# GpSimd takes the layernorm application and the residual-plus-bias sum from VectorE in the stages with heads of 8

## The reference, cut to what matters

```
xn = (x - mean(x)) / sqrt(var(x) + 1e-5)             # over the 128 channels
q  = heads(xn @ Wq + bq)                              # 16 heads of 8
k, v = heads(ctx @ Wk + bk), heads(ctx @ Wv + bv)     # 1601 keys
y  = softmax(q k^T / sqrt(8)) v
out = x + y @ Wp + bp
```

## Time and profile before

| | before |
|---|---|
| timed runs, median | 8038.13 us |
| profiled execution | 8022.59 us, span 8020.8 us |
| PE | 7135.1 us busy, 89% |
| DVE | 5918.4 us, 74% |
| ACT | 4951.6 us, 62% |
| POOL | 2313.2 us, 29% |

### The profile page before, as it was taken

How to read it: one execution, slowest core, us unless ns; L and a number is a source line. 1 busy time by engine, 2 the same in 40 slices (tenths; PEclk the granted TensorE clock), 3 DMA queues, 4 the chain that set the end, 5 groups by cost and what they waited for, 6 DMA issues and landing times. The chain is left out here.

```text
span 8020.8 us, 186125 instructions
## 1 busy us (share of the span) xinstructions
PE 7135.1 (89%) x73814; PEld 3142.3 (39%) x73814; DVE 5918.4 (74%) x12885; ACT 4951.6 (62%) x9846; POOL 2313.2 (29%) x2368
## 2 busy tenths in 40 slices
PE   6999999878999997888599999999998779999979
PEld 2333333353333333444244444444444533333335
DVE  6888888657989996677466666666665469899855
ACT  4778887636888884444255555555554248888852
POOL 1222222111121110444245444544444211221200
PEclk9999999888999998788699999999999779999989
DMA  4444333114433421000100000000000144434400
GB/s 97 101 95 92 83 83 92 45 26 100 99 89 77 99 65 31 15 16 13 53 6 8 7 6 10 6 10 6 7 3 18 49 83 96 96 84 85 97 22 14
DMA packets 319828, 417.80 MB, mean 52 GB/s; under 512 B 56533, under 2 KB 238053, under 8 KB 318968
## 3 DMA queue, kind: packets, MB, share of 16 engines
q1 hardware_dynamic: 317432, 405.36, 22.4%
q10 hardware_dynamic: 1536, 0.53, 0.0%
HBM read 225.41 MB, written 174.66 MB: 50 GB/s over the span
## 5 line engine op out<-in xcount | busy, mean ns | idle before, releaser
L687 ACT ACTIVATE a_probs<-scores_ps 128x512 f32<-128x512 f32 (+2 forms) x5248 | 2821.7, 591 | 356.2 <-PE scores_ps L607 263.4
L746 DVE TENSOR_REDUCE a_unit_max<-bank 128x1 f32<-128x512 f32 x3072 | 2004.0, 684 | 182.0 <-PE bank L594 147.3
L624 PE MATMUL bank<-a_probs,a_v_sb 128*9 128x256 f32 (+1 forms) x20992 | 1614.1, 379 | 29.4 <-ACT a_out_sb L694 20.4
L1275 ACT ACTIVATE cross_probs<-scores_ps 128x512 f32<-128x512 f32 (+1 forms) x1792 | 869.4, 571 | 772.6 <-PE scores_ps L1172 772.6
L1357 DVE TENSOR_REDUCE cross_unit_max<-bank 128x1 f32<-128x512 f32 x1536 | 1006.5, 687 | 319.7 <-PE bank L1158 316.9
L607 PE MATMUL scores_ps<-a_stack 64*128 64x256 bf16 (+1 forms) x10496 | 1131.5, 275 | 61.6 <-ACT a_probs L687 55.8
L1441 POOL TENSOR_TENSOR cross_added<-cross_probs 128x1024 f32<-128x1024 f32 x384 | 902.4, 2350 | 944.6 <-PE bank L1205 868.8
L746 DVE TENSOR_REDUCE a_unit_max<-scores_ps 128x1 f32<-128x512 f32 x1536 | 1050.2, 684 | 162.1 <-PE scores_ps L594 144.6
L594 PE MATMUL bank<-a_stack 63*128 63x512 bf16 (+2 forms) x3413 | 1039.7, 372 | 8.1 <-DMA a_stack<-a_stack_dram 2.6
L607 PEld LDWEIGHTS scores_ps<-a_stack 64*128 64x128 bf16 (+1 forms) x10496 | 373.5, 96 | 991.9 <-ACT a_probs L687 832.8
L594 PE MATMUL scores_ps<-a_stack 63*128 63x512 bf16 (+2 forms) x1707 | 635.9, 373 | 50.8 <-DMA a_stack<-a_stack_dram 47.5
(11 more groups left out here) (421 smaller groups left out, 10119.5 us busy)
## 6 DMA issues: line engine op xcount, KB each, us to landing
a_stack_dram<-a_parts SPq DMA_DIRECT2D x288, 400.2 KB, 4.3
a_stack<-a_stack_dram SPq DMA_DIRECT2D x256, 348.2 KB, 8.0
a_stack<-a_stack_dram SPq DMA_DIRECT2D x128, 444.2 KB, 9.9
a_ctxT<-in_ctxT SPq DMA_DIRECT2D x48, 400.2 KB, 4.9
a_stack_dram<-a_parts SPq DMA_DIRECT2D x288, 64.0 KB, 2.7
a_stack_dram<-a_parts SPq DMA_DIRECT2D x96, 128.0 KB, 2.8
f_x<-x_after_dram SPq DMA_DIRECT2D x32, 256.0 KB, 3.6
x_after_dram<-a_res SPq DMA_DIRECT2D x48, 128.0 KB, 4.6
```

The costliest lines, as they stand in the source:

```text
L624: ins = pe.matmul(out_bank[32 * h:32 * h + V8, q0:TOK], v[0:n, e.t, 4 * e.g + h, :], A.probs[0:n, held, o + q0:o + TOK], start=(e.t == 0), ...
L687: act.activation(by_pair(A.probs[0:n, b, a * 512:(a + 1) * 512])[:, :, q0:TOK], by_pair(score_bank[(2 * e.i + a) % 3][0:n, :])[:, :, q0:TO ...
L746: ins = dve.tensor_reduce(unit_max[:, e.g % 2, qt, 2 * a + j, c:c + 1], bank[:, 0:e.s.chunks[c][1]], AX.X, ALU.max)
L1275: act.activation(probs[0:n, b, h, 0:m, :].rearrange("p m q -> p (m q)"), score_bank[h][0:n, 0:m * TOK], ACT.Exp, scale=scale).then_inc(S[" ...
```

## The change

Two things move from VectorE's list to GpSimd's. `ln_apply` (two instructions of 128x128) is issued by GpSimd at the same event, step 4, between its second and its third `split`. The sum of `x_res` and `b_out` (two instructions of 128x128) is issued by GpSimd at the event `heads_turned`, and a new semaphore `x_res_done` tells VectorE of it. VectorE keeps only the last addition of `proj`. GpSimd's wait for `ln_rstd` moves from behind `ln_rstd` to ahead of `ln_apply`.

```diff
-        S = Sems(nc, ctx, stage, ["ones_in", "ahead_in", "x_res_in", "ln_done", "side_ps", "side_done", "part0", "left",
+        S = Sems(nc, ctx, stage, ["ones_in", "ahead_in", "x_res_in", "x_res_done", "ln_done", "side_ps", "side_done", "part0", "left",
...
-                if e.kind == "ln_apply":
-                    dve.wait_ge(S["ln_rstd"], made + 1)
-                    for t in range(QT):
-                        ins = ln_apply(dve, L, t, xn[:, t, :], x_sb[1 - p][:, t, :])
-                    ins.then_inc(S["ln_done"], 1)
...
                 if e.kind == "proj":
-                    dve.wait_ge(S["x_res_in"], 16 * (prev + 1))
                     if prev >= 1:
                         dve.wait_ge(S["x_out"], 16 * prev)
-                    for t in range(QT):
-                        ins = dve.tensor_tensor(x_res[:, t, :], x_res[:, t, :], W_sb["b_out"][:, :], ALU.add)
-                    chain(ins)
+                    dve.wait_ge(S["x_res_done"], prev + 1)
                     dve.wait_ge(S["side_ps"], e.n + 1)
...
                 if e.kind == "ln_rstd":
                     ln_rstd(pool, S, L, made, QT)
+                if e.kind == "ln_apply":
                     pool.wait_ge(S["ln_rstd"], made + 1)
+                    for t in range(QT):
+                        ins = ln_apply(pool, L, t, xn[:, t, :], x_sb[made % 2][:, t, :])
+                    ins.then_inc(S["ln_done"], 1)
+                if e.kind == "heads_turned":
+                    pool.wait_ge(S["x_res_in"], 16 * e.cur)
+                    for t in range(QT):
+                        ins = pool.tensor_tensor(x_res[:, t, :], x_res[:, t, :], W_sb["b_out"][:, :], ALU.add)
+                    ins.then_inc(S["x_res_done"], 1)
                 if e.kind == "split" and made >= 1:
                     split(pool, e)
```

## The result

The changed kernel takes 8208.22 us in the median of four runs (8197.59 to 8224.91), the kernel before on the same chip 8034.78 us (8025.27 to 8046.97). The ratio is 1.0217, with a 95% interval from 1.0193 to 1.0241. So the kernel is 173 us slower, where +53 us was predicted: the direction was right, the predicted size a third of the real one. One execution of a later kernel (the application ahead of the second split) took 8562.74 us at a mean clock of 0.753, apart from all others; it is counted in that kernel's median of ten and left out of its ratio.

What follows compares the result with a forecast made beforehand. TensorE, 97% busy in `a1`, was taken as the bound. Terms 49.3 + 4.2 + 6.6 - 5 - 2.4 = +52.7 us on 8038.1 us gave 8091 us; eight in ten: 8060 to 8128.

Steps and rivals of the forecast that it cites:

- What bounds the kernel, and where the application lands: TensorE, 97% busy in `a1`, pays waits in full; GpSimd's list is gapless there, so applications stand behind its second split.
- The price of an application: One 128x128 layernorm application on GpSimd: 360 ns taken, with ends of 289 and 746 ns.
- `ln_apply` in `a1` and `a3`: TensorE's transposition of `xn` starts 1.76 us later in 28 segments: +49.3 us.
- the rival of the dear application: GpSimd's application costs 746 ns or more: +85 us, 8123 us; chance 0.14.
- Nothing gives this back: After the late `xn` in `a1` and `a3`, following steps recover none of TensorE's 1.76 us per segment.
- `ln_apply` in `a0`: TensorE starts on `xn` 0.3 us later in 14 segments of `a0`: +4.2 us.
- The residual in `a0`: Sum behind GpSimd's widest `split` delays VectorE's last addition 0.47 us in 14 segments: +6.6 us.
- VectorE's gain on the maxima: In `a1` and `a3` VectorE is free 0.48 us earlier, shortening a wait for a maximum: -5 us, at best -9.5.
- First segments: In the stages' first segments GpSimd is free and `xn` comes earlier: -0.8 us in each of three, -2.4 us.
- VectorE's busy time: Over the whole run, VectorE's busy time falls by about 88 us.

Runs made afterwards that it cites:

- The early application: Changed kernel with GpSimd applying the layernorm right behind `ln_rstd`, ahead of its second split: 8018.55 us, ratio 0.9983 to the kernel before.
- The forms: Changed kernel with GpSimd's application in another form per stage, mean subtraction left out, in `a0` the factor too; computes something else: 8194.52 us.
- the matmuls in the wait: Changed kernel plus useless TensorE matmuls ahead of its wait for `xn` (12 in `a1` and `a3`, 5 in `a0`): 8126.09 us, ratio 1.013.
- the residual alone: Changed kernel with the layernorm application back on VectorE, only the sum of residual and bias on GpSimd: 8031.91 us, ratio 0.9994.

## Why the prediction was wrong in size

- *What bounds the kernel, and where the application lands.* Right. TensorE pays for `xn` in full, GpSimd's list is full at this moment in spite of its 18%, and the third split follows the application directly. The early application shows that only the place counted.
- *The price of an application.* Wrong: 360 ns taken, 818 measured (805 mostly). The bracket of 289 to 746 did not hold it either. I took the middle of the cast and the two-input sum, and the row that should have warned was there: TENSOR_SCALAR of 15 elements at 286 ns. The forms show 390 to 669 ns for simpler relatives of the same instruction, so no neighbouring operation could stand for it.
- *`ln_apply` in `a1` and `a3`.* TensorE's wait is 2.93 us, not 2.1, so 2.93 - 0.34 = 2.59 us late instead of 1.76: 28 x 2.59 = 73 us for 49. With the matmuls in the wait 2.22 of it shows in the segment, which takes in VectorE's gain. This is nearly the rival of the dear application (+85 us in all, where the kernel without the fall of the clock is at +89). Its mechanism was right and I gave it 0.14.
- *"Nothing gives this back".* This is the step that failed. The prediction took a stall at its full length as all that it can cost. In the 12 us behind the wait TensorE ran at 0.57 to 0.72 of its full clock, which adds 3.3 us per segment: 28 x 3.32 = 93 us by the segments of `a1` and `a3`, 82 us by the medians of the whole kernel. The profiled executions of the changed kernel and of that with the useless matmuls differ by 104 us, but the one is the slowest of its four and the other the fastest. The sum of the prediction had no term for the clock and gave no reason for leaving it out. It stood at 1.00 in `a1` in the earlier trace rows, with a wait for `xn` of 0.34 us, and the sum holds only if it stays there.
- *`ln_apply` in `a0`.* +0.3 us per segment was predicted. The wait is 1.33 us, and 0.55 us with one application less on GpSimd. The price makes up the difference. In 8 of 13 of these segments the clock falls too, for three to seven us. The first row is such a one, the second one in which it held:

```profile
582.00:584.00 2.00, 2.00 (x18) 0.90 (x16) 1.90 (x4) 1.33 (x3) 1.66 (x2) 0.51 0.00 0
864.00:866.00 2.00, 1.95 (x22) 0.79 (x24) 1.93 (x5) 1.84 (x4) 1.89 (x3) 1.00 0.00 0
```

- *The residual in `a0`.* Right: 0.47 us per segment predicted. The wait of the next `v_cross` (L643) went from 3.4 to 10.8 us over 14 segments, +0.53 each; by the residual alone the segment grew 0.31. GpSimd and VectorE there:

```profile
969.23 0.87 POOL L809 TENSOR_TENSOR a_x_res<-a_x_res,a_b_out 128x128 f32<-128x128 f32 x2
970.19 0.42 DVE L781 TENSOR_TENSOR a_res<-bank,a_x_res 128x256 f32<-128x256 f32 x1 [1.26 <-POOL a_x_res L809]
```

- *VectorE's gain on the maxima.* Right in sign and near in size: 0.29 x 28 = 8 us by the residual alone, 5 predicted.
- *First segments.* Wrong in sign: TensorE waits 2.1 us there instead of 0.98. `ln_rstd` takes 1.5 us and not 1.1, and the pair of applications 2.12 us, against 0.60 on VectorE before. VectorE does its splits beside it there, and away from them the pair takes 1.59. 3 us instead of -2.4.

```profile
1835.89 2.12 POOL L142 TENSOR_SCALAR a_xn<-a_x,a_ln_mv,a_ln_rs 128x128 f32<-128x128 f32 x2
```

- *VectorE's busy time* fell by 70 us instead of 88: what is left on it takes 18 us more in all.

Summed up in segments: (79.94 - 74.40) x 28 = 155 us in `a1` and `a3`, and (94.29 - 91.83) x 14 = 34 us in `a0`, 189 us. The profiled executions differ by 202 us, the medians by 173. Of the 120 us that the prediction lacks, the clock is 82. The waits give the rest: 0.83 x 28 = 23 in `a1` and `a3`, 1.03 x 13 = 13 in `a0`, 6 in the first segments, less 3 for the maxima, together 39. Their sum of 121 is closer to 120 than these figures are good for, since the profiles give 202 us in all where the medians give 173.

Left open: what sets GpSimd's price by form, why the clock is lower in the untouched stretch when the application alone moves, and what besides its length decides whether the clock falls behind a wait.

## What to carry to other kernels

On an engine that walks a list, a step moved there costs what stands ahead of it at that moment, whatever the engine's mean load says: with the applications behind the second split the kernel was 173 us slower, with them ahead of it no slower than before. A new wait on a TensorE that is otherwise 97% busy must be priced with the clock behind it: here 2.59 us of it cost 5.54 us per segment. Look at the clock of the few us behind a wait, since slices of 200 us hide it, and at every place by itself, since waits of 1.1 to 1.3 us lowered it often at one place and hardly ever at another. An operation of which the trace has no row on its new engine should be measured there first, or bracketed beyond its dearest neighbour.

## What the runs showed of the hardware

- GpSimd's TENSOR_SCALAR of 128x128 in float32 took, in the mean by form: 818 ns (805 in the median) for (x - a) * b with two factors per partition, 669 for the same with constants, 631 for one product with a factor, 390 for a product with a factor and one with a constant. A cast of that size takes 289 ns.
- TensorE's granted clock behind a wait at `x_turned`: in `a1` and `a3` (TensorE otherwise 97% busy) it fell to 0.50 behind waits of 2.93, 2.54 and 2.30 us in every segment, behind 2.15 us in 27 of 28, behind 1.75 us in 20 of 28, behind 0.34 us in none. In `a0` it fell behind 1.33 us in 8 of 13, behind 1.11 us in 9 of 14, behind 0.55 to 0.60 us in none. Behind the wait of 1.27 us at L639 it fell in 4 of 140. It stayed low for three to ten us. Useless matmuls in the wait kept it at 1.00.
- VectorE and GpSimd slow each other. VectorE's two instructions of an application take 870 and 753 ns beside GpSimd's split, 333 to 343 ns where GpSimd is idle. GpSimd's take 1180 and 950 beside VectorE's split in the first segments, 806 and 796 away from it. Behind the split on GpSimd the pair takes 1.59 us, and on VectorE beside the split it took 1.54: the loss comes from what stands ahead of it on the list.
